# A layer of attention, experts and recurrence: the attention's weights go through DRAM and come back repeated

## The reference

```
gains = softmax(q_offset + prior, axis=-1)            # 11 scales a head
for j in range(11):
    d = 1 << j
    for tau, h_coef in enumerate(D4):                 # 4 coefficients
        k_s, v_s = shift(k, d * tau), shift(v, d * tau)
        qk = sum(q * k_s, axis=-1)
        out += gains[j] * h_coef * qk * v_s
out += softplus(bypass) * sum(q * k) * v
return (out * sigmoid(gate)) @ W_out.T + b_out
recurrence:  h = tanh(h @ A.T + x_t @ B.T);  y = h @ C.T
```

## Time and profile before

| | |
|---|---|
| median of 3 runs | 1466.12 us (1459.56 to 1484.78) |
| the profiled execution | 1464.85 us, span of its instructions 1463.1 us |
| PE busy | 1162.0 us (79%) |
| DVE busy | 791.5 us (54%) |
| ACT busy | 651.2 us (45%) |
| POOL busy | 791.0 us (54%) |
| moved by DMA | 107.59 MB, mean 74 GB/s |

### The profile page before, as it was taken

How to read it: one execution, slowest core, us unless ns; L and a number is a source line. 1 busy time by engine, 2 the same in 40 slices (tenths; PEclk the granted TensorE clock), 3 DMA queues, 4 the chain that set the end, 5 groups by cost and what they waited for, 6 DMA issues and landing times.

```text
span 1463.1 us, 32843 instructions
## 1 busy us (share of the span) xinstructions
PE 1162.0 (79%) x9942; PEld 876.2 (60%) x9942; DVE 791.5 (54%) x1723; ACT 651.2 (45%) x2050; POOL 791.0 (54%) x1274
## 2 busy tenths in 40 slices
PE   3878887887978898889987899866998767994481
PEld 2545554565655665666565667765877655884471
DVE  4878898889866776567787567431213201240111
ACT  2233332555445654566544444553553323562241
POOL 2655457655687648754468845875125433323604
PEclk9998987999979997799999578988985567997786
DMA  4700001222221112111123112333322323443442
GB/s 125 208 1 0 1 1 51 67 62 61 80 63 55 56 37 75 43 54 40 45 66 87 43 54 61 99 99 89 99 89 72 93 68 114 118 131 109 124 132 69
DMA packets 117639, 107.59 MB, mean 74 GB/s; under 512 B 15540, under 2 KB 88541, under 8 KB 117469
## 3 DMA queue, kind: packets, MB, share of 16 engines
q1 hardware_dynamic: 106704, 88.01, 21.1%
q0 software_dynamic: 8192, 16.79, 3.9%
q10 hardware_dynamic: 2573, 0.69, 0.2%
HBM read 76.73 MB, written 28.70 MB: 72 GB/s over the span
## 4 chain that ended last, share of the span: by engine, by line
PE 39%; POOL 18%; DVE 13%; issue 10%; another core or an unknown queue 8%; ACT 7%; ACTq 1%; DMA 1%; SPq 1%; DVEq 1%; POOLq 0%
PE bank L1160 9%; PE bank L1147 8%; POOL acc L799 8%; PE bank L1187 5%; POOL mom L764 3%; POOL sorted_x L822 3%; DVE made L1312 2%; DVE term L1341 2%; PE bank L1083 2%; PE bank L1124 2%; PE bank L1051 2%; PE bank L1030 2%; PE bank L1110 2%; PE bank L1140 1%
## 5 line engine op out<-in xcount | busy, mean ns | idle before, releaser
L799 POOL TENSOR_TENSOR acc<-acc,term 128x512 f32<-128x512 f32 x219 | 281.6, 1286 | 71.3 <-DVE term L1341 53.8
L1160 PE MATMUL bank<-w,hT 128*128 x1088 | 214.9, 321 | 22.7 <-ACT hT L985 12.8
L1341 DVE TENSOR_TENSOR term<-bank,V 128x512 f32<-128x512 f32 x251 | 167.9, 684 | 71.3 <-PE bank L1110 43.6
L1005 ACT ACTIVATE hid<-bank 128x16 f32<-128x16 f32 x512 | 93.0, 182 | 253.6 <-PE bank L1187 200.9
L985 ACT ACTIVATE hT<-bank,b1T 128x128 f32<-128x128 f32 x544 | 165.4, 371 | 81.3 <-PE bank L1147 64.8
L1187 PEld LDWEIGHTS bank<-hid,abcT 128*32 128x32 f32 x4096 | 88.3, 116 | 188.1 <-ACT hid L1005 105.5
L839 POOL DMA_INDIRECT back<-sorted_y,slot_i x128 | 125.2, 978 | 138.1 <-DMA sorted_y<-ysb 52.9
L1160 PEld LDWEIGHTS bank<-w,hT 128*128 128x128 f32 x1088 | 172.3, 219 | 40.5 <-issue 35.2
L1187 PE MATMUL bank<-hid,abcT 128*32 128x16 f32 x4096 | 138.0, 200 | 65.5 <-ACT hid L1005 57.8
L1312 DVE SCALAR_TENSOR_TENSOR made<-bank,qkvb,K 128x512 f32<-128x512 f32 x251 | 176.2, 741 | 15.7 <-PE bank L1083 6.8
L1147 PE MATMUL bank<-xTb,w1b 128*128 128x128 f32 x864 | 165.6, 320 | 7.8 <-ACT xTb L973 7.6
(11 more groups left out here) (177 smaller groups left out, 2190.6 us busy)
## 6 DMA issues: line engine op xcount, KB each, us to landing
w1b<-in_W SPq DMA_DIRECT2D x130, 256.0 KB
K<-in_W SPq DMA_DIRECT2D x54, 256.0 KB, 2.7
xsb<-sorted_x SPq DMA_DIRECT2D x184, 64.0 KB
sorted_y<-ysb SPq DMA_DIRECT2D x136, 64.0 KB
X<-in_x SPq DMA_DIRECT2D x64, 64.0 KB
out_x<-X SPq DMA_DIRECT2D x64, 64.0 KB
sorted_x<-K SPq DMA_DIRECT2D x14, 256.0 KB, 3.6
sorted_y<-made SPq DMA_DIRECT2D x48, 64.0 KB
```

The lines of the kernel that those rows point to most:

```text
L799: nc.gpsimd.tensor_tensor(acc[:], acc[:] if k > 1 else term[0][:], term[k % NTERM][:], ALU.add).then_inc(S["terms_added"], 1)
L1005: nc.scalar.activation(hid[n % 2][:, cs], bank[6 + n % 2][:, cs], ACT.Tanh).then_inc(S["h_ready"], 1)
L1160: last = nc.tensor.matmul(bank[SLOT_BANK[place(n)]][:, 0:D], tile(hT[place(n)], c), w2[:, ds(second[n] + c * D, D)], start=(c == 0), stop= ...
L1341: V_.tensor_tensor(term[k % NTERM][:], bank[2 + k % 2][:], V[:, at:at + CW], ALU.mult).then_inc(S["terms_ready"], 1)
```

## The change

It replaces the repetition of the packed weights by PE with a way through DRAM. A packed tile is stored to DRAM by SP ("wstore"), and each shift's 16 rows of 512 columns are read back eight times over into 128 partitions ("fetch"), into a ring of 7 SBUF buffers "spread". DVE multiplies such a buffer by shifted v in place, and POOL adds it. Term 0 still comes from PE, into PSUM bank 1, and is written into acc directly. Banks 2 and 3 are free of weights, so the sums of products of the next chunk wait only for the packs. "high", "low" and "scale" are gone.

The gains are stored with heads innermost, with a zeroed scale ahead. The sum of two neighbouring scales' gains, each with its coefficient, is made on PE: "rows" of group 0 and 2 are pairs of plain matmuls, by the identity and by a scaled identity ("ratio"), in place of DVE's "wshift" and a transpose; the coefficient's remainder goes into "rcopy". Products take their buffers in another turn, so that only products 5 and 6 of a chunk wait for the rows.

At the start, 13 loads count ahead of the derived weights in place of 15; six of them are handed from ACT's queue to SP's, behind the first chunk of x. PE and ACT no longer wait for the whole derivation, and DVE takes the first chunk's statistics before it. The diff, cut:

```diff
-NPROD, NTERM = 7, 4
+NPROD, SPREAD_RING = 7, 7
+
+GAINS_OVERWRITTEN = (5, 6)
...
+def product_buffer(j):
+    return (j + 2) % NPROD
...
-        for g in (0, 2, 1):
-            if g < 2 or g2:
-                piece("ACT", "scale", i, g, 1.1 if g < 2 else 0.25, USUAL, [("gmul", i, 0)])
-        for k in range(TPC):
-            piece("DVE", "wshift", i, k, 0.46, USUAL, [("scale", i, 0)])
-        if g2:
-            piece("DVE", "wshift", i, TPC, 0.32, USUAL, [("scale", i, 2)])
         for g in (1, 0, 2):
             if g < 2 or g2:
-                free = [("low", before, 2 * g + h) for h in range(len(halves(before, g)))] if i and g < 2 else [] if g < 2 else \
-                    [("spread", before, last_term(before, 2)) if i and active(before)[2] else None]
-                piece("PE", "rows", i, g, 0.8, USUAL,
-                      [("scale", i, 1) if g == 1 else ("wshift", i, TPC - 1 if g == 0 else TPC)] + free, bank0=1)
+                free = [("wstore", before, g) if i and (g < 2 or active(before)[2]) else None]
+                piece("PE", "rows", i, g, [2.4, 0.8, 2.0][g], USUAL, [("gmul", i, 0)] + free, bank0=1)
                 piece("ACT", "rcopy", i, g, 0.62, USUAL, [("rows", i, g)], bank0=0)
...
+        for g in range(3 if g2 else 2):
+            piece("SP", "wstore", i, g, 0.1, USUAL,
+                  [("pack2", i, 0) if g == 2 else ("pack", i, g), ("term", i - 2, last_term(i - 2)) if i >= 2 else None], lands=2.6)
         for j, s in enumerate(sums):
-            need = [("product", i, n - 1), ("pack", i, 0)] if j == 0 else \
-                [("low", i, 2 * s.g + s.m // 4)] if s.g < 2 else [("pack2", i, 0)]
-            piece("PE", "spread", i, j, 1.1 if j == 0 or s.g == 2 else 0.52, USUAL,
-                  need + [("pack", i, 1) if j == 1 else None, ("term", i, j - 2) if j >= 2 else None,
-                          ("spread", i, j - 1) if j else None])
-            piece("DVE", "term", i, j, 0.7, USUAL,
-                  [("spread", i, j), ("vcopy", i, 0), ("add", before, last_term(before)) if i else None,
-                   ("xT", i + 1, 0) if j == 3 and i + 1 < CHUNKS else None,
-                   ("add", i, max(1, j - NTERM)) if j >= NTERM else None])
+            if j == 0:
+                piece("PE", "spread", i, 0, 1.1, USUAL, [("product", i, n - 1)])
+            else:
+                f = fetch_of(i, j)
+                piece("SP", "fetch", i, j, 0.1, USUAL,
+                      [("wstore", i, s.g), ("fetch", *fetched_for(f - 1)) if f else None,
+                       ("add", *fetched_for(f - SPREAD_RING)) if f >= SPREAD_RING else None], lands=3.2)
...
+            piece("DVE", "term", i, j, 0.72, USUAL,
+                  [("fetch", i, j) if j else ("spread", i, 0), ("vcopy", i, 0), ("term", i, j - 1) if j else past("out", before)])
...
+        wd = [[nc.dram_tensor(f"weights{g}{u}", (P, CW), F32, kind="Internal").ap() for u in range(2)] for g in range(3)]
...
-        term = [sb(f"term{j}", [P, CW]) for j in range(NTERM)]
-        xn = term[3]
+        xn = sb("xn", [P, CW])
...
+                if c == 0:
+                    for j, n in enumerate(["W_out", "A", "B", "C"]):
+                        sp.dma_start(tile(wload, 4 + j), a[n]).then_inc(S["weights_in"], 16)
+                    sp.dma_start(small[0:NE, 0:D], a["Wg"]).then_inc(S["weights_in"], 16)
+                    sp.dma_start(small[0:32, P:2 * P], a["b1"].rearrange("e (c p) -> (e c) p", p=P)).then_inc(S["weights_in"], 16)
...
+                elif what == "wstore":
+                    if k < 2:
+                        sp.wait_ge(S["packed"], nth("pack", n, k))
+                    else:
+                        sp.wait_ge(S["bank0_taken"], in_turn("reduce2", n))
+                    if n >= 2:
+                        sp.wait_ge(S["terms_ready"], nth("term", n - 2, last_term(n - 2)))
+                    h = H * len(active(n)[k]) if k < 2 else H
+                    sp.dma_start(wd[k][n % 2][0:h, :], wt[k][0:h, :]).then_inc(weights_out[k][n % 2], 16)
+                elif what == "fetch":
+                    s, f = terms(n)[k], fetch_of(n, k)
+                    sp.wait_ge(weights_out[s.g][n % 2], weights_stored(n, s.g))
+                    if f >= SPREAD_RING:
+                        sp.wait_ge(S["terms_added"], nth("add", *fetched_for(f - SPREAD_RING)))
+                    sp.dma_start(spread[f % SPREAD_RING][:],
+                                 bass.AP(wd[s.g][n % 2].tensor, s.m * H * CW, [[CW, H], [0, HD], [1, CW]])).then_inc(
+                                     spread_in[f % SPREAD_RING], 16)
...
-                    elif n:
-                        pool.wait_ge(S["bank0_filled"], in_turn("out", n - 1))
-                    nc.gpsimd.tensor_tensor(acc[:], acc[:] if k > 1 else term[0][:], term[k % NTERM][:],
+                    nc.gpsimd.tensor_tensor(acc[:], acc[:], spread[fetch_of(n, k) % SPREAD_RING][:],
...
-                    nc.scalar.activation(wt[k][0:h, :], bank[0][0:h, :], ACT.Copy).then_inc(S["bank0_taken"], 1)
-                elif what == "high":
-                    g, h = divmod(k, 2)
-                    act.wait_ge(S["packed"], nth("pack", n, g))
-                    if n:
-                        act.wait_ge(S["spread_ready"], nth("spread", n - 1, last_term(n - 1, g)))
-                    own = slice(64 * h, 64 * h + H * halves(n, g)[h])
-                    nc.scalar.activation(spreads[g][h][own, :], wt[g][own, :], ACT.Copy).then_inc(S["high_ready"], 1)
+                    nc.scalar.activation(wt[k][0:h, :], bank[0][0:h, :], ACT.Copy, scale=D4[3] if k == 1 else D4[1]).then_inc(S["bank0_taken"], 1)
...
+                        own, one_less = (gains_tile[c][:, x:x + (P if k < 2 else H)] for x in ((H, 0) if k < 2 else (9 * H, 8 * H)))
+                        if k == 1:
+                            last = nc.tensor.transpose(tile(bank[0], c), own, ident)
                         else:
-                            last = nc.tensor.transpose(bank[0][0:H, c * P:(c + 1) * P], w8[:, c * H:(c + 1) * H], ident)
+                            dst = bank[0][0:P if k == 0 else H, c * P:(c + 1) * P]
+                            nc.tensor.matmul(dst, own, ident, start=True, stop=False)
+                            last = nc.tensor.matmul(dst, one_less, ratio[:], start=False, stop=True)
...
+                    nc.tensor.matmul(bank[1][:], blkw[:], prod[product_buffer(j)], start=True, stop=True).then_inc(S["spread_ready"], 1)
...
+            for place_in_order, (what, n, k) in enumerate(ORDER["DVE"]):
+                if place_in_order == 1:
+                    derive_weights()
...
+                        dst, weights = acc[:], bank[1][:]
+                    else:
+                        u, turn = fetch_of(n, k) % SPREAD_RING, fetch_of(n, k) // SPREAD_RING
+                        dve.wait_ge(spread_in[u], 16 * (turn + 1))
+                        dst = weights = spread[u][:]
+                    V_.tensor_tensor(dst, weights, V[:, at:at + CW], ALU.mult).then_inc(S["terms_ready"], 1)
```

284 lines of the change are left out of this document (113 added, 171 removed).

## The result

| | before | after |
|---|---|---|
| median | 1462.9 us | 1551.16 us (1540.08 to 1573.31) |
| ratio | | 1.0586, 95% interval 1.0503 to 1.0669 |
| span of the profiled execution | 1463.1 us | 1537.9 us |

The change makes the kernel 5.9% slower. The time lies above the range given (1405 to 1540). Some executions of any version fall into a slower state of the chip: the medians here hold them, the ratios leave them out.

What follows compares the result with a forecast made beforehand. The prediction took PE, 88% busy between gates 8 and 15, as the bound there. Changes of +15, -5, +3, -48 and +40 us over the stretches summed to +5: span 1468, time 1470 us, range 1405 to 1540.

Steps and rivals of the forecast that it cites:

- The terms: DVE's multiplications of v, now with two SBUF operands beside POOL's adds: 1.25 us each, bounds 0.68 and 1.67.
- the harmless products: DVE products with PSUM and SBUF operands: beside a POOL add they take their ordinary 0.74 us.
- The start: Startup: SP's opening delays the first DRAM term to 74 us and chunk 0's gate to 93, +15 us.
- PE's work between gates 8 and 15: Chunks 8 to 15: PE busy 391 us, with 52 slots and 237 recurrence steps there.
- The whole-instruction lock: Rival: term and add exclude each other from first to last moment, 1.95 us a pair, 1536 us; chance 0.05.
- I take 85% for PE: 461 us: Gate 8 to gate 15: PE's 391 us at 85% busy gives 461 us against 509, -48.
- DVE becomes the bound: Slower rival: 235 terms cost 276 us per us of term; 2% slower from 1.35 us, 1539 at 1.5; chance 0.18.
- The stretch from gate 4 to gate 8: Four chunk cycles, 48 and three of 49 us, less 5: 190 us against 187, +3.
- The end: After chunk 15's gate: 7 slots and 76 steps more, partly filling a 67 us hole, +40 us.
- SP's queue: Slower rival: fetches wait behind stores and slots' loads behind fetches; 4 us a chunk makes 1534; chance 0.10.
- Faster: Rival: terms slip into POOL's waits at 1.0 us and PE's relief counts at 88% or better: 1420; chance 0.25.
- Nothing changes: Rival: experts and recurrence are the long pole, gains are waited away, within 2%; chance 0.42 together with the forecast.

Runs made afterwards that it cites:

- b_port: Kernel before, every term but term 0 multiplying v by a constant SBUF tile instead of the repeated weights in PSUM: 1527.27 us, ratio 1.0417.
- b_both_port: Kernel before with the change's startup and rows parts, and terms multiplying v by a constant SBUF tile: 1557.17 us, ratio 1.0677.
- a_open_lock: Changed kernel with SP's opening reordered so chunk 0's stores and fetches come earlier, and terms and adds planned as excluding each other: 1469.14 us, ratio 1.0032.
- a_sp_load: Changed kernel with one more 128-byte transfer behind every fetch on SP's queue: 1552.21 us, ratio 1.0626.
- b_both: Kernel before with the change's startup and rows parts, without the way through DRAM: 1491.04 us, ratio 1.0175.
- a_less_fill: Changed kernel with SP's opening reordered, the planner's other numbers, and filler share 0.3 in place of 0.65: 1484.84 us, ratio 1.0157.

## Why the prediction was wrong

**Right by size.** The terms: 1.25 us forecast (bounds 0.68 and 1.67), 1.156 measured; the pair (the two adds of 89.39 take 3.39 us, 1.70 each, against 1.67) and the harmless products stand in the rows of after. The start: 74 us forecast for the first DRAM term and 93 for gate 0, 74.8 and 95.7 measured, with SP in its opening as said. Gate 4: 248 and 252.3. PE's work between gates 8 and 15: 391 us and 396.6; the slots and steps there (52, 237) and behind (108) came out to a step. They were counted from the written order, and two terms of PE's sum, looked up in the traces of that stretch, hold as well (row matmuls 33.6 us more forecast and 33.1 found, fillers 10 and 9.8), so this is not luck. The whole-instruction lock falls: the term of 80.21 ends 0.54 us after the add beside it, as in the earlier trace rows, and not its full 0.68. The Trainium skill, page "SBUF — State Buffer", section "Who interferes with whom", has the loser blocked for the whole instruction: the trace agrees that the two exclude each other, and differs on the last 0.14 us.

**The step that failed** is what comes after these sums: "I take 85% for PE: 461 us". PE's share was 396.55/493.10 = 80%, and the stretch took 493. This is 32 of the 70 us between the forecast (+5) and the result (+74.8). The prediction argued from three engines near 80% in order, and took it that this costs little where PE is the bound. b_port shows what it costs: with PE's instructions and their order unchanged, six tenths of DVE's extra time came through, 59 us, 24 of them in this stretch (533.0 against 509.2). But PE's share does not fall to 80% by the port alone: it is 457.10/533.00 = 86% there, and 84% in b_both_port. It falls where the repetition has left PE as well. From b_both_port to after PE has 43 us less to do in this stretch, and the stretch is 28 us shorter. So dividing PE's work by a share was the wrong way to price it: a shorter list for PE did not pull the stretch with it in full. The rival "DVE becomes the bound" had the right instructions, the terms, and the wrong mechanism and threshold: DVE is only 340.80/493.10 = 69% busy in that stretch, and the rival was to decide from 1.35 us a term, and the run is 5.9% slower at 1.156. Its price, 276 us for each us of term, would make 0.47 us more a term 130 us, where b_port paid 59 for 0.41; the price was too high, and the forecast hid nearly all of it under PE.

**Smaller terms.** The stretch from gate 4 to gate 8 was to take 190 us and took 205: the forecast priced terms and loads there, not the products' wait for the row matmuls (11.1 us in this stretch), which in the order stand behind slots. The end was to grow by 40 us and grew by 59 with the 7 slots and 77 steps that were counted. The stride of the softmax passes was put at nothing, and costs little: the sum over scales takes 1.36 us in place of 0.88, once a chunk, and POOL's multiplication of the gains 1.87 in place of 1.40.

**The premise behind the 85%, the stretch from gate 4 and the end** is that the written order keeps its worth when durations change. The prediction said that the plan takes term and add as independent, and drew from it 85% in place of 88. The runs put 4.1 to 4.4 points on that one omission (2.0 where the plan has SP's numbers too), and 1.1 to 1.5 on SP's opening, which the plan doesn't know either: in a_open_lock, with both mended, more than nine tenths of the loss are gone. How a better order turns into time is shown only in part, by the terms and the products' waits. The rows part, costed as PE records and nothing else, loses 2% alone, and not by those records.

**The rivals.** SP's queue: no (a_sp_load). Faster: only with another order, and then by a percent. Nothing changes: no, though the observation under it holds, since b_both finishes attention 28 us earlier and the run 1.75% later. A rival that was not named is PE's granted clock, whose mean is 0.820 in the profiled execution of after and 0.853 in that of before. It cannot be the main cause: a_less_fill has a lower clock (0.805) and a ratio of 1.0157, and b_both_port a higher one (0.846) and 1.0677.

## What to carry to other kernels

When a kernel's order is written out by a planner, ask of each new instruction which of the planner's assumptions it breaks, a shared port above all, and price that apart from the busy time. Put the exclusion into the planner, beside the durations, before judging the change: here that was worth 2 to 4%, in three pairs of runs, and nothing in the kernel before with the port alone. And an engine that is 68% busy is not cover for more work on it when others wait for its results in order; the b_port experiment, one operand changed and nothing else, measures that in one run.
